# Pixel attention: products of a step grouped by form, maxima of contiguous queries, a sixth key tile added by GpSimd

## The reference, cut to what matters

```
weight = einsum('bct,bcs->bts', q * scale, k * scale)   # [B*8, 1024, 1024]
weight = softmax(weight.astype(float32), axis=-1)
a = einsum('bts,bcs->bct', weight, v)
return x2 + einsum('oc,bct->bot', w_proj, a) + b_proj
```

## Time and profile before

| what | us |
|---|---|
| median of three runs | 2230.95 |
| profiled execution | 2227.61 |
| its span in the trace | 2225.8 |
| TensorE busy (12212 products) | 1979.0 (89% of the span) |
| VectorE busy | 1531.2 (69%) |
| GpSimd busy | 1029.1 (46%) |
| ScalarE busy | 827.0 (37%) |
| mean granted TensorE clock | 0.935 |

### The profile page before, as it was taken

One profiled execution on the slowest core, in us unless ns is written; L12 is line 12 of the kernel. 1 busy time (PEld: TensorE's weight loads), 2 busy tenths in 40 slices (PEclk: granted clock), 3 DMA queues, 4 the chain that ended last, 5 costly groups with the idle time before them and its releaser, 6 DMA issues.

```text
span 2225.8 us, 36373 instructions
## 1 busy us (share of the span) xinstructions
PE 1979.0 (89%) x12212; PEld 1015.5 (46%) x12212; DVE 1531.2 (69%) x2315; ACT 827.0 (37%) x1546; POOL 1029.1 (46%) x437
## 2 busy tenths in 40 slices
PE   6999685799999999999999999999999969888885
PEld 2443232354554554544544544545544335445442
DVE  6766647787666777676777766777666127888786
ACT  0152310004544544443544443544545613333320
POOL 0243210005455355454454444454444608788787
PEclk8799888789999999999999999999999979999996
DMA  7200020232330330330330330330331020122211
GB/s 219 58 2 1 1 85 27 57 115 62 77 77 20 78 79 21 77 79 20 77 79 20 77 79 20 77 79 20 78 77 39 2 97 25 63 65 66 79 46 60
DMA packets 89664, 132.53 MB, mean 60 GB/s; under 512 B 58180, under 2 KB 58486, under 8 KB 89462
## 3 DMA queue, kind: packets, MB, share of 16 engines
q1 hardware_dynamic: 79958, 129.36, 21.1%
q10 hardware_dynamic: 9504, 0.59, 0.3%
HBM read 44.83 MB, written 25.17 MB: 31 GB/s over the span
## 4 chain that ended last, share of the span: by engine, by line
PE 71%; DVE 16%; issue 4%; DMA 4%; ACT 2%; SPq 2%; POOL 1%; POOLq 0%; DVEq 0%; ACTq 0%
PE AV L650 11%; PE S L637 11%; PE RB L621 11%; PE S L621 5%; PE SUM L660 4%; PE RB L689 4%; PE RB L885 3%; DVE MX L1276 3%; SPq L443 2%; PE AV L898 2%; PE RB L766 2%; DVE ENC L1617 2%; DVE DEV L1316 2%; PE RB L706 2%; PE RB L934 1%
## 5 line engine op out<-in xcount | busy, mean ns | idle before, releaser
L1276 DVE TENSOR_REDUCE MX<-RB 128x1 f32<-128x512 f32 x783 | 515.2, 684 | 89.3 <-PE RB L621 80.7
L1014 ACT ACTIVATE PR<-S 128x512 f32<-128x512 f32 x640 | 356.5, 597 | 578.3 <-PE S L637 559.0
L1175 POOL TENSOR_TENSOR ACC<-PR 128x1024 f32<-128x1024 f32 x72 | 170.3, 2373 | 760.6 <-ACT PR L1014 758.7
L637 PE MATMUL S<-QS,KS 98*128 98x512 f32 x1152 | 470.2, 460 | 17.4 <-issue 8.5
L1175 POOL TENSOR_TENSOR ACC<-ACC,PR 128x1024 f32<-128x1024 f32 x152 | 360.0, 2371 | 198.2 <-ACT PR L1014 189.4
L621 PE MATMUL RB<-KS,QS 96*128 96x512 f32 x783 | 393.1, 524 | 32.7 <-DVE MX L1276 20.1
L1014 ACT ACTIVATE X<-S 128x512 f32<-128x512 f32 x512 | 283.7, 597 | 284.0 <-PE S L637 277.2
L621 PEld LDWEIGHTS RB<-KS,QS 96*128 96x128 f32 x783 | 245.0, 318 | 251.6 <-DVE MX L1276 153.0
L637 PEld LDWEIGHTS S<-QS,KS 98*128 98x128 f32 x1152 | 222.4, 198 | 218.5 <-issue 93.6
L1276 DVE TENSOR_REDUCE MX<-S 128x1 f32<-128x512 f32 x369 | 251.7, 682 | 32.2 <-PE S L621 27.0
L621 PE MATMUL S<-KS,QS 96*128 96x512 f32 x369 | 186.3, 505 | 11.4 <-DVE MX L1276 6.8
(11 more groups left out here) (235 smaller groups left out, 2096.3 us busy)
## 6 DMA issues: line engine op xcount, KB each, us to landing
X<-out_y SPq DMA_DIRECT2D x24, 1024.0 KB, 5.1
QS<-HI SPq DMA_DIRECT2D x144, 128.0 KB, 2.4
KS<-HI SPq DMA_DIRECT2D x144, 128.0 KB, 2.5
out_y<-X SPq DMA_DIRECT2D x16, 1024.0 KB, 4.1
QS<-LO SPq DMA_DIRECT2D x72, 128.0 KB, 2.6
KS<-LO SPq DMA_DIRECT2D x72, 128.0 KB, 2.4
X<-in_x SPq DMA_DIRECT2D x8, 1024.0 KB, 8.7
OHU<-out_y SPq DMA_DIRECT2D x8, 512.0 KB, 4.4
```

The lines of the kernel that those rows point to most:

```text
L637: mm(ST[:, (H * s + h) % BANKS, :], KS[par][:, h, P * mt:P * mt + P], QS[par][:, h, HALF * half:HALF * half + HALF], start=True, stop=True ...
L1014: nc.scalar.activation(exps(i, s, pair)[:, HALF * one:HALF * one + HALF], ST[:, (H * s + h) % BANKS, :], ACT.Exp, scale=1.0 if i is None e ...
L1175: nc.gpsimd.tensor_tensor(ACC[:, pair, :], so_far, exps(i, s, pair), ALU.add).then_inc(pool_used, 1)
L1276: nc.vector.tensor_reduce(out=MX[:, h, t, half:half + 1], in_=bank(), op=ALU.max, axis=AX.X).then_inc(ring_free, 1)
```

## The change

GpSimd adds tile 3 too; TensorE's own sums are then for tiles 6 and 7. Tile t of the maxima holds queries 128 t to 128 t + 127. Since the rows are then laid out by tiles, NM (128 x 8) is turned by TensorE into 8 x 128 in a ring bank (`flip`, one job per head, in the step after the head's last maximum), and VectorE makes NMH and NML from that bank. Each row is then a DMA of 8 pieces of 512 bytes. Maxima fill steps 1 to 13, not 1 to 15. In a step TensorE does score, maximum, score, maximum, score, maximum, score, all other maxima, then values, all other jobs, sums. VectorE does the maxima of a step first, then the other jobs.

```
-POOL_TILES = (0, 1, 2, 4, 5)
+POOL_TILES = (0, 1, 2, 3, 4, 5)
-FIRST_SUMMED = 3
+FIRST_SUMMED = 6
...
-        steps = range(1, STEPS)
+        steps = range(1, STEPS - 2)
...
+        done = [s for s in range(STEPS) for job in jobs[s] if job[0] == "max" and job[2:] == (MT - 1, 1)]
+        for h, s in enumerate(done):
+            jobs[s + 1].append(("flip", h))
...
-        NMH = sb("NMH", [P, H, MT], f32r)
+        NMH = sb("NMH", [MT, H, P], f32r)
...
-                        load(QS[par][r:r + 1, h, :].rearrange("o (p t) -> o p t", t=MT).bitcast(f32),
+                        load(QS[par][r:r + 1, h, :].rearrange("o (t p) -> o t p", p=P).bitcast(f32),
...
-                mm(bank(), QS[par][0:3 * D, h, t:N:MT], KS[par][0:3 * D, h, HALF * half:HALF * half + HALF],
+                mm(bank(), QS[par][0:3 * D, h, P * t:P * t + P], KS[par][0:3 * D, h, HALF * half:HALF * half + HALF],
...
+            def flip(u, h):
+                dst = bank()
+                wait(pe, max_ready, H * u + h + 1)
+                nc.tensor.transpose(dst[0:MT, 0:P], NM[:, h, :], IDENT).then_inc(ring_full, 1)
...
-                    scores(u, par, s, (0,))
-                    run(jobs[s][0:1])
-                    scores(u, par, s, (1, 2))
-                    run(jobs[s][1:3])
+                    todo = maxima_of(jobs[s])
+                    for h in range(H):
+                        scores(u, par, s, (h,))
+                        run(todo[h:h + 1] if h < H - 1 else todo[h:])
...
-                    run(jobs[s][3:4])
-                    scores(u, par, s, (3,))
-                    run(jobs[s][4:5])
+                    run(others(jobs[s]))
...
-                    run(jobs[s][5:])
...
+                    nc.vector.tensor_reduce(out=NM[:, h, :], in_=MX[:, h], op=ALU.max, axis=AX.X,
+                                            negate=True).then_inc(max_ready, 1)
+            def flip(u, h):
+                src = bank()[0:MT, 0:P]
+                wait(dve, rows_in[h], 2 * 16 * u)
+                link(nc.vector.tensor_copy(NMH[:, h, :], src))
+                nc.vector.tensor_tensor(NML[:, h, :], src, NMH[:, h, :].bitcast(f32),
+                                        ALU.subtract).then_inc(ring_free, 1)
+                own()
+                dve.sem_inc(negmax_ready, 1)
...
-                    run(jobs[s][0:3])
+                    run(maxima_of(jobs[s]))
...
-                    run(jobs[s][3:])
+                    run(others(jobs[s]))
```

More of the change, by code:

```diff
@@ L152 @@
     START += [[("v", 1)], [("qk", 0, 0)], [("qk", 0, 1), ("qk", 1, 0)], [("qk", 1, 1)]][_h]
+    START += [("flip", _h)]
 def after_jobs():
@@ L165, in first_jobs @@
 def first_jobs():
-    maxima = [("max", h, t, half) for h in range(H) for t in range(MT) for half in range(2)]
+    maxima = []
+    for h in range(H):
+        maxima += [("max", h, t, half) for t in range(MT) for half in range(2)] + [("flip", h)]
     jobs = {("concepts", 1): [("stats",)], ("softmax", 1): [("gn", 0)], ("turn", 1): [("gn", 1)],
@@ L176, in first_jobs @@
         maxima = maxima[n:]
-    return jobs, maxima + [("qk", n // 2, n % 2, 1) for n in range(4)]
+    return jobs, maxima[:-1] + [("qk", n // 2, n % 2, 1) for n in range(4)] + maxima[-1:]
 def program(nc, x, w_l0, w_o, concepts, concepts_t, gammas, conv_w, conv_wt, conv_b, lin1_t, lin2_t,
@@ L721, in run @@
                             max_scores(u + 1, 1 - par, *job[1:])
+                        elif job[0] == "flip":
+                            flip(u + 1, job[1])
                         elif job[0] == "v" and i is None:
@@ L833, in prepare @@
                         max_scores(2, 0, *job[1:])
+                    elif job[0] == "flip":
+                        flip(2, job[1])
             pe.wait_ge(scaled, 1)
@@ L849, in _ @@
                     qk_l0(1, job[1], job[2])
+                elif job[0] == "flip":
+                    flip(0, job[1])
                 else:
@@ L1279, in row_max @@
                     own()
-                    wait(dve, rows_in[h], 2 * 16 * u)
-                    link(nc.vector.tensor_reduce(out=NM[:, h, :], in_=MX[:, h], op=ALU.max, axis=AX.X,
-                                                 negate=True))
-                    link(nc.vector.tensor_copy(NMH[:, h, :], NM[:, h, :]))
-                    nc.vector.tensor_tensor(NML[:, h, :], NM[:, h, :], NMH[:, h, :].bitcast(f32),
-                                            ALU.subtract).then_inc(negmax_ready, 1)
+                    nc.vector.tensor_reduce(out=NM[:, h, :], in_=MX[:, h], op=ALU.max, axis=AX.X,
[8 more added lines that the diff above has]
+                dve.sem_inc(negmax_ready, 1)
             def invert(n):
@@ L1541, in _ @@
                 ring.enter(i - 1, RING_PER)
-                steps.enter(i - 1, 8 + 16 + 6)
+                steps.enter(i - 1, 8 + 16 + 6 - 2 * H)
                 iteration(i, window, None)
```

9 lines of the change are left out of this document (7 added, 2 removed).

## The result

The changed kernel took 2397.5 us (median of four runs, 2395.1 to 2404.1) against 2231.1 for the kernel before on the same chip: a ratio of 1.077, 95% interval 1.071 to 1.082. The forecast was 2328 us, at most 2365. The direction was right, the size was not: the medians are 166 apart, where the forecast had 97 (101 on the profiled execution).

What follows compares the result with a forecast made beforehand. Bound: TensorE's product order, which must leave VectorE time through a three-bank ring. Seven pairs at +14.5 give +101, less 3 for DMAs; window 16 -3, window 17 +6: +101 on 2227.6, so 2328 us, range 2265 to 2365.

Steps and rivals of the forecast that it cites:

- the clock falls too: Rival: waits in steps 2 and 4 of even windows drop TensorE to 1.2 GHz, 14 times 1.3 us: 2346; chance 0.20.
- 1. Bursts of maxima: Steps with maxima in a row wait for VectorE's reductions: six take 4.15 us; odd window, steps 0 to 8, +4.1.
- 2. The fourth score behind the exponent: Steps 0 and 1: the fourth score, now ahead of the values, waits for ScalarE; even window 11.9 against 10.0, +1.9.
- 3. Statistics and group norm: Even windows: statistics delay step 2's maxima, +3.3; GpSimd's additions hold up group-norm operations in steps 3 and 4, +3.5.
- 4 and 6. Steps 5 to 8, 13 to 15: Even steps 5 to 8 +2.1, from late banks and seven maxima; steps 13 to 15, few maxima, -4.1 even, -3.0 odd.
- 5. Steps 9 to 12: Both windows: query and key product closing the step makes a loop of 5.55 us a step; +3.4 and +3.3.
- DMAs: Transfers in SyncE's queue go out some 5 us earlier; 3 us gained in windows 2 to 15, bounds 0 and 8.
- Outside: Window 16 -3, window 17 +6 from GpSimd's longer additions, windows 0 and 1 and stages between 0, bounds -8 and +6.
- Collisions don't grow: Rival: GpSimd finds pauses or loses them to VectorE, returning 3.2 us in each of seven windows: 2305; chance 0.20.
- Strided loads count for nothing: Rival: VectorE bounds the maxima, so shorter weight loads are worth nothing, 14 us lost again: 2342; chance 0.04.
- No change: Rival: only bare bursts and bank waits are real, the group-norm and steps 9 to 12 terms hide: 2238; chance 0.08.
- Faster: Rival: TensorE is the only bound and VectorE catches up, so removed work counts in full, -9.4 a pair: 2160; chance 0.12.

Runs made afterwards that it cites:

- e_fill: Changed kernel plus repeated score products in even windows, 12 in step 2 and 20 in step 4, that compute nothing new: 2382.9 us, 1.069 of before.
- n: Changed kernel, new order kept, with the 1 MB input load moved to the odd window and group-norm operations reading PSUM: 2343.5 us, 1.053 of before.
- m: Changed kernel in the old order, with the 1 MB input load moved to the odd window and group-norm operations reading PSUM: 2177.8 us, 0.981 of before.
- q_tail: m with the new order in steps 9 to 15 of each window only: 2229.0 us, 1.002 of before.
- p_head: m with the new order in steps 0 to 4 of each window only: 2257.4 us, 1.016 of before.
- h_psum: Changed kernel with the group norm's small VectorE operations each given an input in PSUM, one operation more: 2344.0 us, 1.052 of before.
- b_pool: Kernel before with only GpSimd's sixth tile (tile 3) added: 2441.9 us, 1.096 of before.
- c_layout: Changed kernel with the old order of jobs, everything else of the change kept: 2282.1 us, 1.026 of before.
- f_best: Kernel before with the new layout alone: old order, five GpSimd tiles, maxima in steps 1 to 14: 2252.7 us, 1.012 of before.
- a_order: Kernel before with only the new order of jobs: 2410.4 us, 1.084 of before.
- r_six_psum: b_pool with the group norm's small operations reading PSUM; the cast NMH still reads SBUF: 2353.5 us, 1.059 of before.
- k_xin: f_best with the 1 MB load of the next input moved into the odd window, behind XRES: 2233.5 us, 1.005 of before.

## Why the prediction was wrong, point by point

**The step that failed: the clock, put at nothing in the sum and too low in its rival.** The forecast listed "the clock falls too" with a chance of 0.20, at 14 falls of 1.3 us, 18 in all. There are three falls a pair in five of the loop's six, with 20 us of half clock a pair, and others in window 0 and around window 2. The condition of the rival (3 to 5 us of standing still, twice) was in the forecast's own sums; it was priced as if only one value block and ten products ran slowly. Per pair the change takes 9.0 us more than forecast (187.8 against 178.8): steps 0 and 1 +1.9, step 2 +1.4, steps 3 and 4 +2.4, steps 5 to 8 +0.9, odd 13 to 15 +1.2, even 13 to 15 +0.7, the rest 0.4.

The clock makes up 5.0 of the 9.0. In steps 2 to 4 it costs 2.9, by e_fill. Step 0 took 6.6 in window 4, at full clock, against 8.2 at 0.79 in windows 6 to 14: 1.5. Steps 5 to 8 took 29.1 at 0.97, against 28.5 at full clock in e_fill: 0.6. Of the others, 0.9 are the group norm's operations (6.4 where 5.5 stood), 1.9 are steps 13 to 15 (0.9 of that in step 15 of the odd window, up to the next pair's first product, where the forecast had 4.8), and 1.2 lie in many small pieces. At full clock the waits were sized right: steps 2 to 4 take 22.8 in e_fill with 4.9 for the group norm, the forecast had 23.4 with 5.5.

So the clock is some 35 us of the 59 by which windows 2 to 15 exceed their forecast (+157 against +98), the largest term of the miss but not all of it: with it the forecast would have been 2363. Another 15 lie ahead of window 2, below. The pair of the earlier trace rows hid the term: window 6 is one of only two even windows of the loop that have no fall in the kernel before. In windows 4 and 12 step 2 took 8.1 and 7.8 us at a mean clock of 0.81 and 0.78, in window 6 5.0 at 1.00.

**1. Bursts of maxima: right.** Steps of six maxima took 4.14 to 4.17 (4.15 forecast), odd steps 0 to 8 46.1 (45.7).

**2. The fourth score behind the exponent: half.** 13.8 against 11.9. The fall at the start of the pair is most of the difference; n has it too (14.5), m, in the old order, in one of four pairs (10.6). The wait ahead of the pair does not make it by itself: in windows 6, 8 and 10 it is 1.9 to 2.0 us in q_tail without a fall, 1.6 to 2.0 in p_head with one in two of the three. It goes with the new order of the first steps; what in them brings it was not isolated.

**3. Statistics and group norm: the mechanism right, the size nearly.** A wait of 3.48 us for the reduction behind the statistics; the three operations took 6.38 against 5.5, within the bounds of 2.3 and 7.1. h_psum shows them to be worth 5.8 a pair. What the bounds did not have is that one operation can lose to several additions in a row (7.51 and 16.12 in b_pool, 13.79 in c_layout and e_fill); rows 7 shows one each time.

**4 and 6. Steps 5 to 8, 13 to 15:** 29.1 against 28.2; 12.4 and 12.5 against 11.7 and 11.3. Right in kind, short in size.

**5. Steps 9 to 12: right.** 23.3 and 23.3, both as forecast, and at full clock. The new order of these steps costs 6.0 in q_tail; m, which has it not, is 1.9 above before in them.

**DMAs: the credit is missing.** The forecast credited 3 us for transfers that go out earlier. The 1 MB load did, by 3.6 us in window 10, but the wait ahead of the first product was 2.33 against 1.73.

**Outside:** window 16 -3.5 (-3 forecast). Window 17 +6.2 (+6 forecast), by the mechanism forecast: its sums of ACC start 30.4 and 57.5 us into it, before 28.5 and 52.1, and the last one waits for GpSimd:

```profile
1940.59 1.93 PE L691 MATMUL SUM<-ACC,ONES 128*32 128x512 f32 x8 [3.36 <-POOL ACC L1201]
```

Behind it 5.4 came back that the forecast did not have; 4.7 of them are one batch of the last block, which took 47.8 us at a clock of 0.96, and before 52.5 at 0.87. Ahead of window 2 +15.3, 12.2 of it in windows 0 and 1 (0 forecast, bounds -8 and +6). Window 0 takes 72.7 before, 81.6 with the order alone, 82.7 with the sixth tile alone, and 70.3 in m. Window 1 takes 330.6 before, and 334 to 335 in c_layout, f_best and m by the layout, but a_order without it has 335.8 too.

**Rivals.** "Collisions don't grow" is out (1.86, 2.26, 2.26). "Strided loads count for nothing" was not isolated: f_best loses by the start of its pairs, and m, with the short loads, is 4.3 a pair under before with five edits at once. "No change" is out: parts 3 and 5 did not hide, but came at full size. "Faster" is out for this order; the old order with the two repairs is what comes near it.

The parts don't add up. Alone they cost 186 (order), 218 (sixth tile) and 26 (layout), together 166. The layout is what makes the sixth tile bearable, since it takes the copies NMH off GpSimd's path (115.3 us of them in b_pool, 19.6 in c_layout): in the old order 218 become 58.

The forecast said that the page's rule of the shared ports agrees with the rows. The Trainium skill, SBUF — State Buffer (two separate sides), says that whichever starts first keeps the pair for its whole instruction and the other waits until that ends. For h_psum and r_six_psum the rule about two SBUF inputs holds. For NMH, a copy with one input, the page's clause on modes with two ports fits; which mode the copy ran in, no trace shows. But the copy of 7.51 us waited past the ends of three instructions, and the operation of 13.79 us past five; by the measurement the loser can be passed over again.

## What to carry over

Ask of every wait that a change makes not only how long it is but how long the engine then runs at the lower clock, and look in the clock column of a stretch that already waits; here waits of 3.5 and 5.9 us, and the new order at the start of a pair, brought 20 us of half clock a pair. And look at more than one pair: the one that the forecast was built on was without a fall. A new order of jobs is to be judged by what it leaves TensorE to do while the slower engine empties the banks: with the values behind four scores and all maxima there was nothing left. And when a package of edits loses, run each alone and each left out: the sixth tile was the dearest part alone (+218) and belongs to the fastest kernel, once the small VectorE operations beside it have an input in PSUM.

## What the runs showed of the hardware

- A VectorE copy of 0.17 us from SBUF took 7.51 us while GpSimd had additions waiting in a row (b_pool); operations of 0.16 us with two inputs in SBUF took 13.79 (c_layout, e_fill) and 16.12 (b_pool). What decides whether one gets in after one addition (2.3 us) or after several was not settled.
- Products that compute nothing new, put into waits, made the kernel faster: 224 of them, windows 2 to 15 shorter by 24 us, half clock 48 us instead of 140.
- Behind the jump to a loop's next turn TensorE stood still with no releaser in the trace: 1.7 us before and 1.8 in m, 4.7 in c_layout, and twice in f_best (1.9 and 4.7) and k_xin (1.6 and 2.4). Loads of program code of 8 and 16 KB lie in the DMA queues there. The Trainium skill, Runtime: NRT & Kernel Launch (Instruction fetch mechanics), says that a taken branch to a target outside the two pages held forces that page to be fetched by DMA before the engine goes on. The place agrees with it. That the second wait was shorter without the 1 MB load (2.4 against 4.7) does too; that the change has the load and no second wait is not explained by it. No run took the code loads themselves away, so it stays an explanation that was argued.
- Weights read with a step of eight elements (96x128, before) loaded in 0.32 us, contiguous ones (the change) in 0.20.
